# Attention's product of query features with the state: 32x32 diagonal tiles instead of 64x64

## The reference, cut to what matters

```python
def favor(x, omega):                      # x: B, S, 16 heads, 8
    dh = x.shape[-1]
    m = 2 * omega.shape[-1]               # 8 features
    xs = x * dh ** (-0.25)
    u = jnp.einsum('bshd,dm->bshm', xs, omega)
    h = 0.5 * jnp.sum(xs * xs, axis=-1, keepdims=True)
    return jnp.concatenate([jnp.exp(u - h), jnp.exp(-u - h)], axis=-1) * m ** (-0.5)

def step(carry, qkv):                     # for each token
    Sst, zst = carry
    qi, ki, vi = qkv
    Sst = Sst + ki[..., :, None] * vi[..., None, :]
    zst = zst + ki
    num = jnp.einsum('bhm,bhmd->bhd', qi, Sst)
    den = jnp.einsum('bhm,bhm->bh', qi, zst) + ATTN_EPS
    return ((Sst, zst), num / den[..., None])
```

## Time and profile before

| | us |
|---|---|
| median of 3 runs | 1832.27 |
| lowest, highest | 1825.32, 1837.38 |
| span of the profiled execution | 1828.0 |
| PE busy, whole span | 1571.7 |
| DVE busy, whole span | 1443.5 |
| ACT busy, whole span | 935.3 |
| POOL busy, whole span | 698.6 |

### The profile page before, as it was taken

How to read it: one execution, slowest core, us unless ns; L and a number is a source line. 1 busy time by engine, 2 the same in 40 slices (tenths; PEclk the granted TensorE clock), 3 DMA queues, 4 the chain that set the end, 5 groups by cost and what they waited for, 6 DMA issues and landing times.

```text
span 1828.0 us, 65037 instructions
## 1 busy us (share of the span) xinstructions
PE 1571.7 (86%) x27934; PEld 1150.5 (63%) x27934; DVE 1443.5 (79%) x3906; ACT 935.3 (51%) x1958; POOL 698.6 (38%) x620
## 2 busy tenths in 40 slices
PE   6777365399969999999999999999999999999853
PEld 4344254399946677776667777666677667777542
DVE  4998566766658888888888888888888988888864
ACT  4887476366524444445544444554444544444373
POOL 0777636345513234215224323423321522431354
PEclk9888655599969999999999999999999999999876
DMA  9730012333200000000000000100000000000437
GB/s 264 145 100 1 21 50 90 97 102 101 83 13 14 3 9 9 15 3 14 15 3 13 16 3 8 20 3 9 9 15 3 14 15 3 11 6 3 109 102 233
DMA packets 88606, 79.69 MB, mean 44 GB/s; under 512 B 22416, under 2 KB 77040, under 8 KB 88064
## 3 DMA queue, kind: packets, MB, share of 16 engines
q1 hardware_dynamic: 70736, 46.17, 9.6%
q0 software_dynamic: 10848, 25.70, 4.9%
q10 hardware_dynamic: 6736, 3.66, 0.7%
HBM read 46.74 MB, written 34.01 MB: 44 GB/s over the span
## 4 chain that ended last, share of the span: by engine, by line
PE 50%; DVE 13%; ACT 4%; issue 2%; DMA 1%; DVEq 1%; POOL 0%; another core or an unknown queue 0%; POOLq 0%; ACTq 0%
PE psum L1965 8%; PE psum L1890 8%; PE psum L1859 4%; PE psum L1868 4%; PE psum L1928 2%; PE psum L1934 2%; PE psum L1882 2%; PE psum L1936 2%; PE psum L1875 2%; PE psum L1937 2%; PE psum L1938 2%; PE psum L1948 2%; PE psum L1847 2%; DVE at_kb L1543 2%; PE psum L1929 2%
## 5 line engine op out<-in xcount | busy, mean ns | idle before, releaser
L1890 PE MATMUL psum<-attn_w,at_qa 128*128 128x128 f32 x1536 | 197.6, 282 | 0.0
L1752 POOL TENSOR_TENSOR at_xres<-at_xn,attn_rows 128x512 f32<-128x512 f32 x32 | 40.9, 1277 | 394.2 <-DVE at_xn L368 394.2
L1965 PE MATMUL psum<-at_vT,attn_w 128*128 128x512 f32 x384 | 180.6, 614 | 6.8 <-ACT at_vT L1697 5.8
L1890 PEld LDWEIGHTS psum<-attn_w,at_qa 128*128 128x128 f32 x1536 | 179.6, 192 | 6.1 <-issue 0.7
L1543 DVE TENSOR_SCALAR at_kb<-at_kf,const 128x512 f32<-128x512 f32 x192 | 178.4, 989 | 0.0
L1757 POOL TENSOR_TENSOR at_xn<-at_sqk,attn_rows 128x512 f32<-128x512 f32 x48 | 63.6, 1326 | 202.8 <-DVE at_sqk L368 202.8
L1549 DVE STREAM_TRANSPOSE at_vb<-at_vT 32x512 uint32<-32x512 uint32 x192 | 134.7, 701 | 1.9
L1669 ACT ACTIVATE at_qa<-at_qf,const 128x512 f32<-128x512 f32 x192 | 127.6, 714 | 1.6
L1713 ACT ACTIVATE at_qa<-psum,attn_bf 128x512 f32<-128x512 f32 x192 | 122.1, 678 | 10.6 <-PE psum L1965 5.4
L1565 DVE TENSOR_TENSOR at_weights<-psum,const 128x1024 f32<-128x1024 f32 x96 | 115.6, 1204 | 11.3 <-PE psum L1859 11.3
L361 ACT ACTIVATE at_rstd<-at_mv,const 128x4 f32<-128x4 f32 x96 | 28.1, 292 | 184.3 <-DVE at_mv L349 184.2
(11 more groups left out here) (308 smaller groups left out, 3884.2 us busy)
## 6 DMA issues: line engine op xcount, KB each, us to landing
ex_rows<-sorted_x SPq DMA_DIRECT2D x71, 129.0 KB
ti_rows<-tile_rows SPq DMA_DIRECT2D x8, 640.0 KB
x<-in_L_attn_x SPq DMA_DIRECT2D x8, 512.0 KB, 7.3
tile_rows<-in_L_attn_x SPq DMA_DIRECT2D x8, 512.0 KB
x<-token_y POOLq DMA_DIRECT2D x8, 512.0 KB
tile_y<-ti_rows SPq DMA_DIRECT2D x16, 192.0 KB
out<-x ACTq DMA_DIRECT2D x12, 256.0 KB
expert_w<-in_L_ffn_w SPq DMA_DIRECT2D x1, 2048.0 KB, 14.2
```

Of the source, the lines that this page charges most:

```text
L1890: last = mm(bank(f.s, 1)[:, c * D:(c + 1) * D], hidden[f.s][:, t, c * P:(c + 1) * P], k.w2[:, f.l, t, :], start=(t == 0 and c == 0), stop= ...
L1965: mm(bank(f.s, c), k.w1[:, f.l, c * P:(c + 1) * P], hT[f.s][:], start=True, stop=True).then_inc(hid_ready, 1)
```

## The change

`carried` now has four matmuls a block instead of two. Each takes one head group: stationary are its 32 features of the 32 tokens (`qf`, unmasked; the other groups' features are on other partitions and take no part), moving is the state on these 32 partitions, and the output goes to the 32 partitions of that group, so the four tiles lie on the diagonal of the array. The sums are the same, without the products with zero. `qa` is still made, for the scores. Order, waits and `start` flags stay.

```diff
                 def carried(s):
 
                     for g in range(NSUB):
-                        for h in two:
-                            mm(bank(1 - s, 2 + g // 8)[half_of(h), g % 8 * GW:(g % 8 + 1) * GW], qa[s][half_of(h), g, 2 * h:2 * h + 2, :].rearrange("p a i -> p (a i)"),
-                               state[s][half_of(h), :, g], start=(g % 8 == 0), stop=False, skip_group_check=True)
+                        for a in range(HQ):
+                            mm(bank(1 - s, 2 + g // 8)[quad(a), g % 8 * GW:(g % 8 + 1) * GW], qf[s][quad(a), block_of(g)],
+                               state[s][quad(a), :, g], start=(g % 8 == 0), stop=False, skip_group_check=True)
```

## The result

| | before | after |
|---|---|---|
| median of the runs, us | 1833.74 | 1926.99 |
| lowest, highest | 1825.32, 1837.38 | 1925.61, 1935.04 |
| ratio, with its 95% interval | | 1.0523 [1.0489, 1.0556] |
| span of the profiled execution | 1828.0 | 1924.0 |

The change makes the kernel 93 us slower. (The kernel before has one run more here than at the head of the document, hence 1833.74.) The forecast had the same sign and half the size: 1880 us, +48. The measured time lies 2 us above the end of the forecast range.

The account below looks back on a forecast made before the run. The prediction took PE to bind most attention slots: 24.34 us plus 0.11 of drain and 1.45 of instruction stops gives 25.90 against a mean 24.88, +48 us over 47 to 48 slots, 1832 + 48 = 1880 us; range 1848 to 1925.

Parts of the forecast that it names:

- What bounds the kernel: In attention's 48 slots PE binds most, at 24.34 us; a PE delay beyond 25.3 us a slot counts in full everywhere.
- Part 1, the product: Streaming of L1868: twice the records, four tiles at a time, 2.14 us against 2.24; taken as no change.
- same-bank rival: In the product L1868, tiles writing one bank take turns: 4.27 us, +1.70 a slot, 1912 us in all; chance 0.08.
- the stride: L1868's moving operand lies 17 floats apart; this was held to make each record 47 ns too long.
- Part 2, the drain: One more change of tile shape, between second scores L1859 and product L1868: 0.11 us a slot.
- Part 3, the stops: In dense work PE waits for instruction blocks, 256 records every 3.4 to 3.9 us: 1.45 us a slot; chance 0.74.
- The sum: PE-bound slot: 24.34 + 0.11 + 1.45 = 25.90 us; against the mean 24.88, +1.02, over 47 to 48 slots +48 us.
- DVE slots: Some 14 attention slots with VectorE on the chain, about 1 us longer each, 25.3 us; a 25.90 slot was to exceed them.
- longer turn of the instruction queue: Slower arrival of PE's instruction blocks than assumed; one reason for stretching the range's upper end from 1911 to 1925.

Follow-up runs that it names:

- e2: Changed kernel with the product of head groups 1 and 3 left out (72 records a slot in place of 128, output wrong): 1839.1 us, ratio 1.0066.
- e4: Kernel before with the product's moving operand read contiguously, not 17 floats apart (multiplies other numbers, output wrong): 1826.09 us, ratio 0.9989.
- e6: Changed kernel with half of the sums (L1847) left out, 32 matmuls a slot ahead of the dense stretch, output wrong: 1915.25 us, ratio 1.0486.
- e7: Changed kernel with half of the weighted values (L1875) left out, 32 matmuls a slot inside the dense stretch, output wrong: 1874.12 us, ratio 1.0234.
- g1: Changed kernel with the first half of the product issued before the second half of the feed-forward output, nothing left out: 1909.64 us, ratio 1.0435.
- f3: Kernel before with the busy delay of e8 and four POOL operations cut from 512 to 32 columns: 1847.38 us, ratio 1.0283, +46 over f1.
- e8: Kernel before with six useless 128-column matmuls between product and weighted values, PE kept busy 1.37 us more a slot: 1904.13 us, ratio 1.0423.
- f1: Kernel before with four POOL tensor operations cut from 512 to 32 columns, output incomplete, base for the like kernels: 1801.77 us, ratio 1.0015.
- f4: Kernel before with PE idling for four small ScalarE operations (0.99 us a slot) and four POOL operations cut as in f1: 1836.76 us, ratio 1.0217.
- f2: Changed kernel with the same four POOL operations cut to 32 columns as in f1: 1879.16 us, ratio 1.0443, +77 over f1.
- e10: Kernel before with POOL's outcome chain (L1763 to L1769) put behind the next slot's L1752 and L1753: 1885.61 us, ratio 1.0313.

## Why the prediction was half right

- **What bounds the kernel**: right. PE sets the slot; a delay of it reached the end in every experiment that had one.
- **Part 1, the product**: right in size. 2.24 us before and after, 32x32 tiles four at a time. The same-bank rival (4.27 us, +80) came near in time, 1912, and is false: e2 and the row of 128 records in 2.24 us refute it. What the Trainium skill (TensorEngine Tiling (Array Packing), Gotcha 1) says of it, that different row tiles cannot access one bank at the same time, does not hold for these tiles. The reason I gave, the stride, is only partly right: e4 took it away and 27 of the 47 ns stayed. What the rest is, no run tells.
- **Part 2, the drain**: right. 0.11 us a slot, 5.0 us in the table.
- **Part 3, the stops**: right. I took 1.45 us a slot in all. Measured: the dense stretch grew by 58.7 / 46 = 1.28 on top of the 0.23 or so of before (11 us over 47 slots), thus 1.51. Some 9 us of it are not stops but work at the lower clock behind them (below), so the stops alone are nearer 1.3, an estimate. Queue 8 went from 197 to 218 packets (221 forecast), with starts 3.2 to 4.3 us apart around the stops. e2, e6, e7 and g1 show the cause: what counts is how many instructions stand in the dense stretch. The Trainium skill's "mostly hidden" (Runtime: NRT & Kernel Launch, Instruction fetch mechanics) doesn't hold for a stream of such short matmuls.
- **The sum**: this step failed. I wrote that a slot of 25.90 is "above the 25.3 of the DVE slots, so all slots take it", and "Nothing moves on ACT, DVE or POOL". So the sum put at nothing what a longer and uneven slot of PE sets off, a late VectorE and a lower clock. The measured mean slot is (1806.6 - 550.2) / 47 = 26.73 us where the sum had 25.90: 0.83 a slot, 39 us too little.

Where the 39 us are:

- 8 us are the first slot alone. PE waits 3.2 us in it for VectorE in both traces, and it lasted 29.9 us before and 33.6 after. I had spread its length over 14 "slots of the DVE kind" and let it shrink to 25.90.
- 31 us are in the other 46. In the table's terms the sum had 5 us of drain and 46 x (1.45 - 0.23) = 56 of stops, less 9 of today's waits that the longer slot hides: 52. Measured are 5.0, 58.7 and -7.7. So the hiding worked nearly as forecast, and the stops were 3 us more. But 27 us came on top, for which the sum had no term:

1. *VectorE beside POOL, about 15 us.* L1952 waits for the late L368 (+9.9), and the first scores wait for L1553 (+5.4): at each of the five waits there PE resumes 0.10 us after L1553 has ended, though the profile puts them down to `issue`, and in front of each L1543's four operations last 5.5 to 6.7 us beside four of POOL's. When PE's slot changes, the hand-written orders of VectorE and POOL shift against one another, and tensor_scalar operations that ran alone land beside POOL's. With less POOL work in the same places, a busy PE delay costs 46 us and not 77 (f3 against e8), and the longer pairs vanish. For the change itself the same comparison gives 93 - 77 = 16 us (1.0 per cent by the ratios, with intervals of about 0.35 on each side); it is rough, since f1 has a collision of its own.
2. *Half clock after stops, about 12 us here and 9 in the dense stretch.* In the slow stretches of the changed kernel the starts of records lie 20.6 us further apart, in sum, than the median for records of the same line; before there is nothing of this in the 46 slots. 9 of the 20.6 fall into the dense stretch; the others make most of the +6.4, +3.9 and +1.6 of the table. The slots of f4 give a like price, 8 us for seven stretches.

The two causes also mix, since a late VectorE makes PE idle and slow work stands behind the idle place (row 731.82 above), so the shares are estimates. That a delay sets off both is shown by e8 against f3 and by f4. Why f2 has larger stops than the changed kernel (70.2 against 58.7 us in the dense stretch) no experiment tells.

The range ended at 1925 for want of these terms. That it ended so near to the measured 1927 is no merit: it had been stretched for a longer turn of the instruction queue and for half of the bank rival, and neither came true.

No version beat the kernel before: e4 ties with it, and g1 is the best of those that compute the whole new product.

## What to carry to other kernels

Count instructions, not only their time: on TensorE here, blocks of 256 instruction records came 3.2 to 4.3 us apart. The dense stretch used up a block in 2.77 us before and stopped in a third of the slots; at 2.26 us it stopped more than once a slot. So cutting this matmul into more tiles of the same total time only cost, and spreading the short ones among wide ones gave part of it back (1.0523 to 1.0435). When a delay is added to the engine that binds, don't take off the waits of today without asking what else moves: let a kernel with a plain busy delay of that size measure it (here 1.37 us a slot cost 77 us, not 42). And a stop cost more than its length where the clock stood lower after it.

## What was unexpected in the hardware

- TensorE's clock stood at its lower level after single stops of 0.7 us (f4) to 2.0 us (f2) in a stream that was otherwise over 90% busy, while most stops of that size left it alone (61 stops, 58.6 us, between 600 and 1790 us; 12 slow stretches). Busy delays of 1.37 us in every slot (f3) brought none in 46 slots, idle ones (0.68 us of each 0.99) seven.
- A VectorE tensor_scalar of 128x512 takes 0.47 us alone and up to 2.58 us beside POOL's tensor_tensor; of 128x128, 0.33 us alone and up to 2.10.
- Beside POOL's scatter, short matmuls stopped 0.47 us after every four or so (e10); cause open.
